# A Mamba and attention block on one core: where VectorE reads ScalarE's tanh and softplus jobs, and in which slots the step size jobs stand

## What is computed

```python
xz = rmsnorm(x, rms_w) @ in_proj                       # 256 -> 2 * 512
xi, z = split(xz)
xi = silu(causal_conv(xi, conv_w, 4 taps) + conv_b)
dt, Bm, Cm = split(xi @ x_proj, [16, 16, 16])
delta = softplus(dt @ dt_w + dt_b)                     # (B, L, 512), the step size
h = exp(delta_t * A) * h + delta_t * x_t * B_t         # for each t, h is (512, 16)
y = sum over the 16 states of h * C_t, + xi * D
out = x + (y * silu(z)) @ out_proj
```

## Time and profile before

| | us |
|---|---|
| median of 3 runs | 578.59 |
| lowest and highest of them | 576.77, 580.87 |
| the profiled execution, whole | 581.45 |
| its span, first to last instruction | 579.3 |
| mean granted TensorE clock in it | 0.926 of 2.4 GHz |

### The profile page before, as it was taken

The page is one execution under the profiler, slowest core; times in us unless marked ns, Lnnn a source line. Parts: engine busy times, 40 slices in busy tenths (PEclk is TensorE's granted clock), DMA queues, the critical chain, the costliest instruction groups (busy, mean ns, idle before and its releaser), DMA issues.

```text
span 579.3 us, 7844 instructions
## 1 busy us (share of the span) xinstructions
PE 481.0 (83%) x2753; PEld 339.3 (59%) x2753; DVE 485.7 (84%) x569; ACT 352.5 (61%) x612; POOL 357.9 (62%) x215
## 2 busy tenths in 40 slices
PE   8968998789668999796689998966897867889992
PEld 6424664465457666554566665545785555878651
DVE  4779989987999899989998999799999989861512
ACT  3765666678765667886757768877466557521210
POOL 5039699747884698777856987787567548100001
PEclk9979999857999999979999999799998879699997
DMA  9331011110111011111110110111111860019004
GB/s 292 101 112 36 37 37 37 39 38 36 37 36 37 36 39 40 36 37 37 38 36 26 48 40 37 37 37 36 38 37 37 294 259 1 1 47 369 13 1 150
DMA packets 17918, 38.87 MB, mean 67 GB/s; under 512 B 1665, under 2 KB 10497, under 8 KB 17874
## 3 DMA queue, kind: packets, MB, share of 16 engines
q1 hardware_dynamic: 17874, 38.32, 19.0%
HBM read 36.08 MB, written 2.23 MB: 66 GB/s over the span
## 4 chain that ended last, share of the span: by engine, by line
PE 36%; DVE 33%; issue 16%; ACT 7%; POOL 6%; DVEq 0%; POOLq 0%; ACTq 0%
DVE scanmem L1686 19%; DVE yTd L1702 8%; PE hT L794 6%; PE pp L508 5%; POOL scanmem L1353 5%; PE pp L532 4%; PE pp L592 3%; PE yacc L566 3%; PE dA L765 2%; PE pp L558 2%; ACT hc L1227 2%; DVE yTd L1611 1%; PE pp L736 1%; PE yacc L562 1%; PE pp L664 1%
## 5 line engine op out<-in xcount | busy, mean ns | idle before, releaser
L1353 POOL TENSOR_TENSOR scanmem<-par,scanmem 128x1024 f32<-128x1024 f32 x128 | 299.1, 2362 | 94.7 <-PE hT L794 59.8
L1217 ACT ACTIVATE dA<-par,Aneg 128x512 f32<-128x512 f32 x256 | 172.5, 690 | 71.3 <-DVE scanmem L1686 70.2
L794 PE MATMUL hT<-con,scanmem 128*128 128x128 f32 x1024 | 158.7, 293 | 60.5 <-DVE yTd L1702 36.8
L794 PEld LDWEIGHTS hT<-con,scanmem 128*128 128x128 f32 x1024 | 122.0, 149 | 118.7 <-DVE yTd L1702 49.0
L1686 DVE TENSOR_TENSOR_SCAN scanmem<-dA,carry,scanmem 128x512 f32<-128x512 f32 x128 | 156.9, 1269 | 2.5 <-ACT dA L1217 2.4
L1686 DVE TENSOR_TENSOR_SCAN scanmem<-dA,scanmem 128x512 f32<-128x512 f32 x128 | 149.2, 1208 | 3.4 <-ACT dA L1217 3.0
L1227 ACT ACTIVATE hc<-hT,CTs 128x512 f32<-128x512 f32 x128 | 87.2, 681 | 78.1 <-PE hT L794 77.6
L1702 DVE SCALAR_TENSOR_TENSOR yTd<-hT,CTs,yTd 128x512 f32<-128x512 f32 x120 | 87.9, 733 | 10.9 <-PE hT L794 10.7
L566 PE MATMUL yacc<-con,hc 128*128 128x128 f32 x512 | 77.1, 293 | 5.8 <-ACT hc L1227 5.8
L566 PEld LDWEIGHTS yacc<-con,hc 128*128 128x128 f32 x512 | 63.2, 151 | 10.0 <-ACT hc L1227 6.5
L508 PE MATMUL pp<-xnT,wi 128*128 128x512 f32 x120 | 63.1, 658 | 5.1 <-ACT xnT L993 3.2
(11 more groups left out here) (194 smaller groups left out, 487.8 us busy)
## 6 DMA issues: line engine op xcount, KB each, us to landing
scanmem<-brow SPq DMA_DIRECT2D x32, 512.0 KB, 3.6
par<-in SPq DMA_DIRECT2D x1, 4096.0 KB, 18.1
scanmem<-in SPq DMA_DIRECT2D x1, 4096.0 KB, 15.1
xt<-in SPq DMA_DIRECT2D x4, 512.0 KB, 6.5
wi<-in SPq DMA_DIRECT2D x2, 1024.0 KB, 6.7
out<-par SPq DMA_DIRECT2D x4, 512.0 KB, 4.1
aw<-in SPq DMA_DIRECT2D x5, 256.0 KB, 6.6
xr<-in SPq DMA_DIRECT2D x1, 1024.0 KB, 8.8
```

Of the source, the lines that this page charges most:

```text
L794: last = nc.tensor.transpose(hT[:, i % 2, m * P:(m + 1) * P], hb[:, n % RING, m, i * P:(i + 1) * P], ident)
L1217: A(dA[:, m % 2, :], delta(c)[:, m, :], ACT.Exp, scale=Aneg[:, m * NS + s:m * NS + s + 1]).then_inc(da_ready, 1)
L1353: nc.gpsimd.tensor_tensor(hb[:, n % RING, ms, :], dx(c)[:, ms, :], Bb[:, row:row + 1, :].to_broadcast([P, 2, T]), ALU.mult).then_inc(bx_re ...
```

## The change

Three things. VectorE's reads of V and D jobs go from the end of half h to half h + 1, between its first and its second scan (`read_late`); Z and all other jobs are read where they were (`read_by_vector`). In `PROLOGUE` D1 and D2, which shared slot 20, get slots 20 and 21, and D3 and the four Z go one slot later. GpSimd's multiplies of delta by x go one state later. On ScalarE jobs and exps keep their places towards each other; only the slots differ.

```diff
--- before.py
+++ after.py
@@ -51,8 +51,8 @@
 
 
 PROLOGUE = {3: [("T", 0), ("T", 1)], 4: [("I", 0)], 5: [("I", 1)], 6: [("I", 2)], 7: [("I", 3)], 8: [("V", 0)],
-            10: [("V", 2)], 12: [("V", 3)], 14: [("X", 0)], 18: [("XT", 0), ("D", 0)], 20: [("D", 1), ("D", 2)], 21: [("D", 3)],
-            22: [("Z", 0)], 23: [("Z", 1)], 24: [("Z", 2)], 25: [("Z", 3)]}
+            10: [("V", 2)], 12: [("V", 3)], 14: [("X", 0)], 18: [("XT", 0), ("D", 0)], 20: [("D", 1)], 21: [("D", 2)], 22: [("D", 3)],
+            23: [("Z", 0)], 24: [("Z", 1)], 25: [("Z", 2)], 26: [("Z", 3)]}
 EPILOGUE = {1: [("Y", 1), ("Y", 3)], 11: [("O", 0)], 16: [("O", 1)], 28: [("R", 0)], 30: [("R", 1)]}
 LAST_EPILOGUE = {1: [("Y", 1)], 2: [("Y", 3)], 3: [("O", 0)], 5: [("O", 1)], 17: [("R", 0)], 19: [("R", 1)]}
 ATT = [6, 8, 8, 10, 12, 14, 15, 16, 17, 20, 22, 23, 24, 27]
@@ -62,7 +62,8 @@
 POOL_TILE = 1
 POOL_AT = [4, 5]
 SCALING_AT = 3
-DX_AT = [13, 14]
+DX_AT = [14, 15]
+LATE = ("V", "D")
 POOL_TANH_AT = 11
 POOL_FINISH_AT = 7
 
@@ -144,6 +145,16 @@
 def to_read(h):
 
     return BESIDE[h - 1] if h else []
+
+
+def read_by_vector(h):
+
+    return [job for job in to_read(h) if job[0] not in LATE]
+
+
+def read_late(h):
+
+    return [job for job in to_read(h - 1) if job[0] in LATE] if h else []
 
 
 
@@ -1705,18 +1716,22 @@
                 for s in range(NS):
                     n = c * NS + s
                     scan_step(n, 0)
+                    for job in read_late(2 * n):
+                        read(job)
                     scan_step(n, 1)
                     if n:
                         mac_step(n - 1, 1)
-                    for job in to_read(2 * n):
+                    for job in read_by_vector(2 * n):
                         read(job)
                     scan_step(n, 2)
+                    for job in read_late(2 * n + 1):
+                        read(job)
                     scan_step(n, 3)
                     if n:
                         mac_step(n - 1, 3)
                     if s == 0 and c:
                         gate_even(c - 1)
-                    for job in to_read(2 * n + 1):
+                    for job in read_by_vector(2 * n + 1):
                         read(job)
                     if c == 0:
                         batch1_rows(s)
```

## The result

The changed kernel takes 587.87 us (median of 20 runs, 581.76 to 591.25) against 580.06 us (20 runs of the kernel before beside it, 575.11 to 582.26). The ratio is 1.0127, 95% interval 1.0101 to 1.0153: slower by 1.3%, some 7.4 us. The profiled execution took 591.12 us with a span of 589.0 us, 9.7 us above the span of before, at a mean granted clock of 0.900 where the 20 runs have 0.908.

A forecast was written before the change was run, and what follows sets the result against it. It took TensorE (83% busy) and VectorE (84%) both to have little slack, with 14.5 us of waits at reads as the prize. V reads +1.2 and slots +4.4 made +5.6 us: 584.2 us on the median 578.59, range 576 to 590.

The forecast's parts named there:

- The scan waits for the exp in place of the read for the job: At stalled reads the scan still waits for ScalarE's exp; the read loses its cover, costing +0.6 us each.
- V reads: Moved V reads, passes 0 to 2: -0.5 us in pass 0, +0.25 and +0.6 in each other pass, sum +1.2.
- D stage: Step size jobs one to a slot: later Z0, longer half clock, +1.7 us in passes 1 and 2, +1.0 in pass 0.
- The replay of pass 1: Hand replay from half 20 at 240.66 with traced durations: half 25 later by +0.2 to +3.3 us depending on the clock, +1.7 taken.
- the double wait: Two jobs no longer share a slot, so this wait goes, with TensorE's 0.88 us wait for the bank D3 needs.
- Half clock 13 to 14 us in passes 1 and 2: Sign of being right: TensorE at half clock some 3 us longer per pass, where it was 10.24 us in pass 1.
- rival C: TensorE at half clock until Z0 is done in each pass: +11.1 us, 589.7 us; chance 18%.
- Stages after the Z jobs and the tail as long as before: Sign of being right: no change in time in the stages behind the Z jobs and at the end.
- Rival B: The moved reads hide VectorE's waits, the exp being ready in time: up to 14.5 us go, 564.1 us; chance 10%.
- Rival A: TensorE's clock comes back early or does not fall: +1.8 us, 580.4 us, down to 576 with some double wait gained; chance 27%.
- The weighed rule: Transposes don't bring TensorE's clock to full, so only Z0 could raise it: the +3.3 us case in each pass.

The follow-up runs named there:

- e4: The changed kernel with ScalarE's first exp of the next half issued ahead of the V and D jobs instead of behind them: 576.06 us, ratio 0.9938.
- e7: e4 with six unused identity products on TensorE ahead of each D of passes 1 to 3: 575.1 us, ratio 0.9932.
- e12: e4 with two unused identity products on TensorE ahead of each D of passes 1 to 3: 573.42 us, ratio 0.991.
- e2: The kernel before with only the V reads moved behind the first scan, old slots, D reads where they were: 575.88 us, ratio 0.9941.
- e1: The changed kernel with VectorE's V and D reads put back at the end of the half, new slots and later GpSimd products kept: 578.93 us, ratio 0.9978.
- e3: The changed kernel with the V reads put back, D reads still moved, in the new slots: 582.39 us, ratio 1.0034.
- e10: The changed kernel with two unused identity products on TensorE ahead of each D of passes 1 to 3: 582.84 us, ratio 1.0032.
- e8: e4 with the V and D reads back in their old places, so new slots and the exp ahead: 587.66 us, ratio 1.0148.

## Why the prediction was right

Forecast +5.6 us (584.2), measured +7.4 by the ratio (587.87 against 580.06): right in direction and mechanism, within its range of 576 to 590, a little small. Of the 3.7 us between 584.2 and 587.87, 1.5 are the base, 578.59 by 3 runs and 580.06 by 20. By its steps:

- *The scan waits for the exp in place of the read for the job.* Right, shown by 22.7 us before scans (5.9 before) and 0.0 before the moved reads, and from the other side by the exp ahead, which takes that wait away: 11.8 us less in e4, 8.4 and 9.4 us less where the clock was nearly level (e7, e12).
- *V reads, -0.5 and twice +0.85, bounds -0.6 and +2.4.* Measured -0.66, +0.69 and +0.64: sum +0.7 in place of +1.2, the same in e2. By halves, 9 to 12 (V0, V2) came to +0.17 and +0.13 in passes 1 and 2 and 13 to 16 (V3) to +0.54 and +0.51, against 0.25 and 0.6. In pass 0 halves 17 and 18 took 0.3 us more in the changed kernel and in e2, not in e1 and e3, which halves the gain there.
- *D stage, +1.7 in passes 1 and 2, +1.0 in pass 0.* Measured +1.76, +2.04 and -0.29: +3.5 in place of +4.4. The replay of pass 1 had half 25 at 263.0 from a half 20 at 240.66, 22.3 us; it took 22.55. What I filed under the slots does not come of the slots alone: these (e1) cost +0.15 a pass in passes 1 and 2 and win 0.8 in pass 0. In pass 0 I weighed only the loss by half clock, which was there already, and not what the double wait gives back.
- *Half clock 13 to 14 us in passes 1 and 2.* It was 17.07, 3 to 4 us more, since it began at 242.67, 0.8 us behind the start of half 20, where it was 3.3 us behind before, and the clock came back 2.0 us into Z0 (257.72) and not as Z0 began; rival C had it back only behind Z0. The D stages of passes 1 and 2 were still only 0.1 and 0.3 us longer than forecast.
- *Stages after the Z jobs and the tail as long as before.* Wrong in this profile: 3.3 us more from pass 3 on, at a clock of 0.89 where it was 0.91, and two short stretches at half clock at the starts of passes 1 and 2, +0.3 and +0.6. But the same code from pass 3 on took 176.4 (e2, e10) to 183.3 us, so of this term one profile says little, and no run shows what sets it.
- V and D stages together make +4.2 us where 5.6 were forecast. The other 3.2 of the 7.4 lie where the forecast had nothing, so that the total came nearer than its terms is luck. Which stages hold them in a usual run is open: by the mean clocks the changed kernel has 109 - 89 = 20 us more at half clock, and in the one trace its D stages have 12 more ((17.7 - 19.6) + 6.9 + 6.9), but that trace is among the slowest of its 20 runs.

Rival B (the waits are hidden) asked for ScalarE's exp to be ready; e4 supplies that, and then V reads wait no more and D reads 5.4 us in place of 10.5, though the gain on before is 0.6% and not 14.5 us. Rival A is ruled out by the clock: 17.07 us at half in passes 1 and 2, not less than 10.24. The weighed rule, that of the Trainium skill in "TensorE: Matmul & The Clock Gate", Part 4: PE-mode transpose, on transposes and the clock, would have given 589.7; the time lies between it and the forecast. The stretch of before that speaks against the rule stands, and no run here tested the rule by itself.

## What to carry to other kernels

When an engine waits for another's result, look at what that other engine does next for it: a wait can be the cover of a second dependence queued behind the first, and moving the wait then only exposes the second. Look at both queues together (here reads behind the scan and the exp ahead of the job); with the new slots, the reads alone cost 1.5% (changed kernel against e1), the exp alone 1.5% (e8 against e1), and both together took 0.5% off (e4 against e1). The V reads alone in the old slots (e2) were 0.6% faster than before, by a higher clock in other stages and not by their own, which grew by 0.7 us. And put numbers on a moved instruction at each site: where other work stood beside the wait (the count of pass 0) it was a gain, where nothing did it was a loss of up to its own length: 0.5 us of 0.6 at V3, 0.1 to 0.2 at V0, where TensorE's queue bounds.

## What was not expected of the hardware

- The same instructions in the same order took 35.75 us with 10.2 us of half clock and 33.66 us with 3.4 us (D stage of pass 2, before and e2), and 37.21 against 33.65 with 19.6 and 6.8 (pass 0): 0.31 and 0.28 us for each microsecond of half clock. In pass 1, with 10.2 and 17.1 us, it was 36.21 against 36.67, only 0.07: what half clock costs depends on where in the stage it falls.
- A change of 0.7 us in another stage (e2) moved the mean clock of all runs from 0.923 to 0.930 and the time by -3.4 us by the ratio. Two effects of VectorE's order are therefore not to be added: V reads alone -3.4 us, on top of the D reads +5.5 us.
- Two small products ahead of each D, in its own bank, raised the mean clock by 0.018 to 0.028 (0.923 to 0.942, 0.908 to 0.936, 0.923 to 0.941). Six raised it a little more, and had the higher median in all three pairs (585.36 and 577.36, 583.52 and 582.84, 575.1 and 573.42), though the intervals of the last two pairs overlap.
